# Spreading the softmax reciprocals across partitions on TensorE instead of through DRAM, with the low-half cast moved earlier on GpSimd

## The reference, cut to what matters

```
q = (x @ Wq).reshape(B, S, N_HEADS, HEAD_DIM).transpose(0, 2, 1, 3)
k = (x @ Wk).reshape(B, S, N_KV_HEADS, HEAD_DIM).transpose(0, 2, 1, 3)
v = (x @ Wv).reshape(B, S, N_KV_HEADS, HEAD_DIM).transpose(0, 2, 1, 3)
q = q * cos + _rotate_half(q) * sin
k = k * cos + _rotate_half(k) * sin
q = q * xscale
k = k * (1.0 / xscale)
scores = jnp.einsum('bhqd,bhkd->bhqk', q, k) / scale
scores = jnp.where(causal[None, None], scores, -jnp.inf)
attn = jax.nn.softmax(scores, axis=-1)
out = jnp.einsum('bhqk,bhkd->bhqd', attn, v)
return out @ Wo
```

## Time and profile before

| | us |
|---|---|
| median of 3 runs | 757.99 |
| lowest, highest | 755.96, 760.92 |
| the profiled execution, device time | 760.92 |
| its span, first to last instruction | 758.1 |

### The profile page before, as it was taken

One profiled execution on the slowest core, in us unless ns is written; L12 is line 12 of the kernel. 1 busy time (PEld: TensorE's weight loads), 2 busy tenths in 40 slices (PEclk: granted clock), 3 DMA queues, 4 the chain that ended last, 5 costly groups with the idle time before them and its releaser, 6 DMA issues.

```text
span 758.1 us, 16144 instructions
## 1 busy us (share of the span) xinstructions
PE 610.7 (81%) x4354; PEld 395.9 (52%) x4355; DVE 539.3 (71%) x1555; ACT 468.7 (62%) x1269; POOL 529.3 (70%) x396
## 2 busy tenths in 40 slices
PE   3567749787988888898879888888776799999992
PEld 1244425444555555555545555555453577777761
DVE  6967749877888787888878888788755254333378
ACT  3685456656768576686765867658574674555542
POOL 4574657988787787877878678797988893554510
PEclk9988979999999999999999999999997799999996
DMA  9366966658465574655756557565688773665773
GB/s 306 93 139 157 225 165 140 118 130 182 101 129 125 114 149 101 132 118 117 142 108 125 119 118 140 114 133 116 112 160 189 217 145 73 145 139 138 194 289 106
DMA packets 251448, 109.29 MB, mean 144 GB/s; under 512 B 213556, under 2 KB 236564, under 8 KB 251412
## 3 DMA queue, kind: packets, MB, share of 16 engines
q1 hardware_dynamic: 247300, 98.32, 59.9%
q0 software_dynamic: 3840, 10.52, 4.6%
q10 hardware_dynamic: 272, 0.02, 0.0%
HBM read 41.49 MB, written 19.09 MB: 80 GB/s over the span
## 4 chain that ended last, share of the span: by engine, by line
POOL 20%; PE 19%; DMA 16%; issue 15%; ACT 10%; SPq 10%; DVE 9%; ACTq 1%; POOLq 0%; DVEq 0%
DMA stage<-rinv_dram 10%; PE bank L1591 9%; POOL stage L604 8%; PE bank L1621 6%; POOL arena L590 4%; SPq L471 4%; ACT arena L844 4%; SPq L473 3%; ACT stage L864 3%; DMA arena<-stage 3%; POOL arena L597 3%; DVE bank L1174 2%; PE bank L1600 2%; SPq L477 2%; POOL compare L646 2%
## 5 line engine op out<-in xcount | busy, mean ns | idle before, releaser
L604 POOL TENSOR_TENSOR stage<-arena,stage 128x1280 bf16<-128x1280 f32 x64 | 167.3, 2614 | 10.2 <-DMA arena<-stage 8.5
L844 ACT ACTIVATE arena<-bank,nmax 128x384 f32<-128x384 f32 (+2 forms) x320 | 147.1, 475 | 32.1 <-DVE nmax L1161 31.7
L597 POOL TENSOR_TENSOR arena<-arena 128x512 bf16<-128x512 f32 x80 | 92.3, 1161 | 99.0 <-ACT arena L829 98.9
L1457 PE MATMUL bank<-arena 128*128 128x512 f16 (+7 forms) x768 | 120.9, 308 | 23.8 <-POOL arena L597 21.9
L1426 PE MATMUL bank<-xnT_hi,arena 128*128 (+1 forms) x320 | 114.7, 401 | 29.3 <-DVE arena L1148 25.6
L1487 PE MATMUL bank<-arena 128*128 (+2 forms) x768 | 104.1, 286 | 34.3 <-DVE arena L1152 27.4
L1471 PE MATMUL bank<-arena 128*128 128x512 f16 (+7 forms) x768 | 119.1, 306 | 6.3 <-DMA arena<-stage 6.3
L1161 DVE CUSTOM_DVE_ANT_0 bank<-bank,mask_b 128x512 f32<-128x512 f32 (+3 forms) x256 | 119.3, 524 | 0.0
L1487 PEld LDWEIGHTS bank<-arena 128*128 (+2 forms) x768 | 77.6, 102 | 67.2 <-issue 27.4
L1174 DVE TENSOR_TENSOR bank<-bank,stage 128x512 f32<-128x512 f32 x64 | 68.9, 1077 | 56.9 <-DMA stage<-rinv_dram 55.2
L590 POOL TENSOR_TENSOR arena<-arena 128x512 f32<-128x512 f32 x77 | 98.3, 1286 | 10.6 <-DVE arena L1148 10.3
(11 more groups left out here) (146 smaller groups left out, 1102.3 us busy)
## 6 DMA issues: line engine op xcount, KB each, us to landing
stage<-rinv_dram SPq DMA_DIRECT2D x64, 256.0 KB, 3.4
xs_dram<-s_sb SPq DMA_DIRECT2D x12, 516.0 KB, 5.1
stage<-w_gate_up SPq DMA_DIRECT2D x16, 352.0 KB
arena<-ys_dram SPq DMA_DIRECT2D x8, 512.0 KB, 6.7
stage<-w_down SPq DMA_DIRECT2D x16, 176.0 KB
stage<-wq SPq DMA_DIRECT2D x4, 512.0 KB, 7.5
stage<-wo SPq DMA_DIRECT2D x4, 512.0 KB, 7.7
arena<-stage SPq DMA_TRANSPOSE x128, 3.5
```

What stands on the lines that cost most here:

```text
L597: pool.tensor_tensor(dst, rot_a[buf], hi, ALU.subtract).then_inc(rot_lo, 1)
L604: pool.tensor_tensor(p_lo, probs[par], p_hi, ALU.subtract).then_inc(probs_lo, 1)
L844: return act.activation(dst, src, ACT.Exp, scale=-1.0, bias=nmax[:, par, qt:qt + 1], accum_out=rsum[:, par, to:to + 1])
L1457: ins = pe.matmul(score_bank[u][:, col:col + n_k], qT[a][:, j * S + qt * P:j * S + (qt + 1) * P], kT[m][:, 0:n_k], start=(n == 0), stop=(n ...
```

## The change

The reciprocals no longer go through DRAM. TensorE transposes each of their four columns, broadcast over 128 columns, against the identity into a PSUM bank of its own (`rinv_bank`, bank 4), which leaves all 512 reciprocals in every partition; ScalarE copies the bank to the one buffer `inverse`; `scale_output` then reads bank and buffer with stride one. The two DMAs of a head and their waits are gone from SyncE. `invert_sums` moves into the rope, behind its first product. `p_lo` becomes two buffers, so `low_probs` waits for the transposition two heads back. On GpSimd `low_probs` moves ahead of the rotation's low half, for head 3 also ahead of the sum of k, and for head 0 ahead of the low half of q2; the low half of k moves behind the loop over heads.

```diff
-        p_hi, p_lo = halves[0].bitcast(F16), halves[1].bitcast(BF16)
-        inverse = [stage[:, KEPT + PCOLS + n * S:KEPT + PCOLS + (n + 1) * S] for n in range(2)]
+        p_hi, p_lo = halves[0].bitcast(F16), [half.bitcast(BF16) for half in halves[1:]]
+        inverse = stage[:, KEPT + 3 * PCOLS // 2:KEPT + 3 * PCOLS // 2 + S]
...
-            def load_inverse(rd, j):
-                h = rd.head(j)
-                sp.wait_ge(rinv_out[j % 2], rd.landed(j))
-                if h == 0:
-                    sp.wait_ge(w_lo, W_FIRST)
-                if h >= 2:
-                    sp.wait_ge(o_scaled, h - 1)
-                sp.dma_start(inverse[j % 2], rinv_dram[j % GH:j % GH + 1, :].to_broadcast([P, S])).then_inc(inverse_in[j % 2], 16)
...
                 sp.dma_start_transpose(pT[par][0].rearrange("p (g t) -> p g t", t=P), p_hi).then_inc(hi_in[par], 16)
-                sp.wait_ge(inverted, h + 1)
-                sp.dma_start(rinv_dram[j % GH].rearrange("(p q) -> p q", q=QT), rinv[:, j % GH, :]).then_inc(rinv_out[par], 16)
-                if h > 0:
-                    load_inverse(rd, j - 1)
                 sp.wait_ge(probs_lo, h + 1)
...
             def low_probs(rd, j):
                 h, par = rd.head(j), j % 2
                 pool.wait_ge(probs_hi, h + 1)
-                if not isinstance(h, int) or h >= 1:
-                    pool.wait_ge(lo_in[1 - par], rd.landed(j - 1))
-                pool.tensor_tensor(p_lo, probs[par], p_hi, ALU.subtract).then_inc(probs_lo, 1)
+                if not isinstance(h, int) or h >= 2:
+                    pool.wait_ge(lo_in[par], rd.landed(j) - 16)
...
+                pool.tensor_tensor(p_lo[par], probs[par], p_hi, ALU.subtract).then_inc(probs_lo, 1)
...
+                    low_probs(rd, j + 1)
                     if j == 2 and not rd.last:
                         rotate_sum("k", rd.item("k"))
...
-                    if j == 2 and not rd.last:
-                        rotate_lo("k", rd.rot("k"))
-                    low_probs(rd, j + 1)
...
                 if not rd.last:
+                    rotate_lo("k", rd.rot("k"))
                     rotate_sum("q2", rd.item("q2"))
...
+                    low_probs(rd, GH)
                     rotate_lo("q2", rd.rot("q2"))
-                    low_probs(rd, GH)
...
+            def spread_inverse(rd, j):
+                h = rd.head(j)
+                act.wait_ge(spread_ps, h + 1)
...
+                    act.wait_ge(o_scaled, h)
...
+                act.copy(inverse, rinv_bank[:]).then_inc(spread, 1)
...
                     exponentials(rd, j + 1)
+                    if j > 0 or not rd.first:
+                        spread_inverse(rd, j - 1)
...
                     rotate_hi("k", rd.rot("k"))
+                spread_inverse(rd, 2)
                 output_hi(rd, 2)
...
                 dve.tensor_tensor(rot_a[buf], ps[:], tab[:, cos, :], ALU.mult)
                 half = DH // 2
+                if inverted_head is not None:
+                    invert_sums(*inverted_head)
...
-                dve.wait_ge(inverse_in[j % 2], rd.landed(j))
+                dve.wait_ge(spread, rd.head(j) + 1)
                 dve.wait_ge(pv, rd.head(j) + 1)
-                o = o_bank[j % 2][:].rearrange("d (q p) -> d q p", q=QT)
-                dve.tensor_tensor(o, o, inverse[j % 2].rearrange("d (p q) -> d q p", q=QT), ALU.mult).then_inc(o_scaled, 1)
+                dve.tensor_tensor(o_bank[j % 2][:], o_bank[j % 2][:], inverse, ALU.mult).then_inc(o_scaled, 1)
...
+            def spread_inverse(rd, j):
+                h = rd.head(j)
+                pe.wait_ge(inverted, h + 1)
+                if not isinstance(h, int) or h >= 1:
+                    pe.wait_ge(spread, h)
+                for qt in range(QT):
+                    ins = pe.transpose(rinv_bank[:, qt * P:(qt + 1) * P], rinv[:, j % GH, qt:qt + 1].to_broadcast([P, P]), ident_f[:])
+                ins.then_inc(spread_ps, 1)
...
                     score(rd.head(j + 1), j + 1, queries[j + 1], None, True)
+                    if j > 0 or not rd.first:
+                        spread_inverse(rd, j - 1)
...
                     project(rd, "q2")
+                spread_inverse(rd, 2)
```

More of the change, by code:

```diff
@@ L257, in build @@
         stage = sb("stage", [P, ERING * WE], F32)
-        halves = [stage[:, KEPT + n * (PCOLS // 2):KEPT + (n + 1) * (PCOLS // 2)] for n in range(2)]
-        p_hi, p_lo = halves[0].bitcast(F16), halves[1].bitcast(BF16)
-        inverse = [stage[:, KEPT + PCOLS + n * S:KEPT + PCOLS + (n + 1) * S] for n in range(2)]
+        halves = [stage[:, KEPT + n * (PCOLS // 2):KEPT + (n + 1) * (PCOLS // 2)] for n in range(3)]
+        p_hi, p_lo = halves[0].bitcast(F16), [half.bitcast(BF16) for half in halves[1:]]
+        inverse = stage[:, KEPT + 3 * PCOLS // 2:KEPT + 3 * PCOLS // 2 + S]
         shared_s = [sb("shared_hi", [P, SHARED_W], F16), sb("shared_lo", [P, SHARED_W], BF16)]
@@ L319, in build @@
         bank = [ctx.enter_context(nc.psum_tensor(f"bank{n}", [P, 512], F32)) for n in range(8)]
-        score_bank, o_bank, misc_bank = bank[0:3], [bank[3], bank[5]], bank[6:8]
+        score_bank, o_bank, rinv_bank, misc_bank = bank[0:3], [bank[3], bank[5]], bank[4], bank[6:8]
         gu_bank, hT_bank, y_bank = bank[0:2], bank[2:4], bank[4:6]
@@ L471, in transpose_probs @@
                 sp.dma_start_transpose(pT[par][0].rearrange("p (g t) -> p g t", t=P), p_hi).then_inc(hi_in[par], 16)
[L472 to L475 removed]
                 sp.wait_ge(probs_lo, h + 1)
[L477 removed]
+                sp.dma_start_transpose(pT[par][1].rearrange("p (g t) -> p g t", t=P), p_lo[par]).then_inc(lo_in[par], 16)
             xs_tiles = xs_dram.rearrange("(t p) d -> p t d", p=P)
@@ L601, in low_probs @@
                 pool.wait_ge(probs_hi, h + 1)
-                if not isinstance(h, int) or h >= 1:
-                    pool.wait_ge(lo_in[1 - par], rd.landed(j - 1))
-                pool.tensor_tensor(p_lo, probs[par], p_hi, ALU.subtract).then_inc(probs_lo, 1)
+                if not isinstance(h, int) or h >= 2:
+                    pool.wait_ge(lo_in[par], rd.landed(j) - 16)
+                if isinstance(h, int) and h == 1:
+                    pool.wait_ge(w_lo, W_FIRST)
+                pool.tensor_tensor(p_lo[par], probs[par], p_hi, ALU.subtract).then_inc(probs_lo, 1)
             rotate_lo("q0", PROLOGUE.rot("q0"))
@@ L966, in _ @@
             round_(Round(NG - 1, "last"))
+            spread_inverse(EPILOGUE, -1)
             output_hi(EPILOGUE, -1)
@@ L1167, in invert_sums @@
                 dve.wait_ge(totalled, h + 1)
+                if not isinstance(h, int) or h >= GH:
+                    dve.wait_ge(spread_ps, h + 1 - GH)
                 dve.reciprocal(rinv[:, j, :], rsum[:, par % 2, 0:QT]).then_inc(inverted, 1)
             def scale_output(rd, j):
-                dve.wait_ge(inverse_in[j % 2], rd.landed(j))
+                dve.wait_ge(spread, rd.head(j) + 1)
                 dve.wait_ge(pv, rd.head(j) + 1)
-                o = o_bank[j % 2][:].rearrange("d (q p) -> d q p", q=QT)
-                dve.tensor_tensor(o, o, inverse[j % 2].rearrange("d (p q) -> d q p", q=QT), ALU.mult).then_inc(o_scaled, 1)
+                dve.tensor_tensor(o_bank[j % 2][:], o_bank[j % 2][:], inverse, ALU.mult).then_inc(o_scaled, 1)
             def output_lo(rd, j):
@@ L1187, in add_projection, with first_rope @@
                                   ALU.add).then_inc(misc_free, 1)
-            def first_rope(name, freed=None):
-                rotate_products(name, PROLOGUE.item(name), PROLOGUE.bank(name), freed, ROT_BUF_PROLOGUE)
+            def first_rope(name, freed=None, inverted_head=None):
+                rotate_products(name, PROLOGUE.item(name), PROLOGUE.bank(name), freed, inverted_head, ROT_BUF_PROLOGUE)
             dve.wait_ge(tab_in, 16)
@@ L1228, in round_, with rope @@
                     freed["q0"], freed["k"] = PROLOGUE.rot("q0"), PROLOGUE.rot("q2")
-                def rope(name):
+                def rope(name, inverted_head=None):
                     if not rd.last:
-                        rotate_products(name, rd.item(name), rd.bank(name), freed[name])
+                        rotate_products(name, rd.item(name), rd.bank(name), freed[name], inverted_head)
+                    elif inverted_head is not None:
+                        invert_sums(*inverted_head)
                 for j in range(GH - 1):
@@ L1241, in round_ @@
                             first_rope("q3", PROLOGUE.rot("q1"))
-                        rope("q0")
+                        rope("q0", (h, j + 1))
                         if not rd.first:
@@ L1251, in round_ @@
                             x_items_lo(rd, X_BEFORE[j])
-                        rope(("q0", "q1", "k")[j])
+                        rope(("q0", "q1", "k")[j], (h, j + 1))
                         if not rd.first:
@@ L1281, in round_ @@
                     tile_experts(1)
-                rope("q3")
-                if not rd.last:
```

(2 more changed lines are left out.)

16 lines of the change are left out of this document (7 added, 9 removed).

## The result

| | before | after |
|---|---|---|
| median, us (runs side by side on one chip, 4 of each) | 758.06 | 777.80 |
| lowest, highest | 755.96, 760.92 | 776.34, 781.62 |
| profiled execution; its span | 760.92; 758.1 | 778.42; 776.6 |
| mean granted TensorE clock | 0.946 | 0.938 |
| read from HBM, MB | 41.49 | 24.72 |

The ratio of after to before is 1.0266, with a 95% interval of 1.0212 to 1.0319: slower by 2.7%. The forecast was 763, its range ended at 774. The DMA work did go away, and the time rose all the same.

The account below looks back on a forecast made before the run. No engine is full; a chain of handovers bounds the round. Rounds 0 to 3 -2.5, rounds 4 to 13 +10, round 14 +0.2, round 15 -2.6: +5.1, on the median 763 us; range 740 to 774.

Parts of the forecast that it names:

- a, row maximum 0 to 1: VectorE in a loop round: the reciprocal inside the rope makes it stand 0.5, so 4.93 becomes 5.4 us.
- b, row maximum 1 to 2: VectorE: ScalarE's copy comes when the DMA did; `scale_output` saves 0.4, the reciprocal 0.1; 8.83 becomes 8.3 us.
- c, to `p_lo` 2: Row maximum 2 to `p_lo` 2 on GpSimd: no rotation or landing ahead, 6.36 becomes 4.8 us, 1.6 won.
- d, `p_lo` 2 to the end of low k: GpSimd runs without waits; low q0 (1.1) and `p_lo` 3 (2.6) added ahead of the keys, 9.77 becomes 13.5 us.
- e, to the next row maximum 0: From low k's end: row maximum 0 follows the scores without the wait for DRAM, 1.05 instead of 2.15 us.
- Rival 2: TensorE's clock halves at head 0's scores each round after 2.2 idle: +6.5 to +15, say 773 us; chance 0.12.
- rounds 0 to 3: Opening rounds: 4.0 won in round 1, 1.5 lost in rounds 1 to 3; net -2.5, bounds -4.0 and +3.
- The 4.0 of round 1: Start of round 1: loads leave SyncE some 8 us earlier, so ScalarE's 4.02 stand for a transposition is won.
- rival 3: The early gain does not come, transpositions still queue behind the loads: +4 on the forecast, 767 us; chance 0.07.
- round 14 and the end: Round 14: GpSimd's extra casts lie in slack, +0.2. Round 15: earlier `p_lo` 1 and expert loads, -2.6.
- Rival 1: GpSimd's longer queue finds slack, TensorE's own list sets a round of 30.8: 740 us; chance 0.24.
- Rival 4: Handovers are 1 us a round shorter in all than added up: 753 us, within 1%; chance 0.09.

Follow-up runs that it names:

- the first experiment: The changed kernel with the low half of head 3's probabilities back behind the low half of k on GpSimd, all rounds but the last: 743.66 us, ratio 0.9784.
- the slots' run: The changed kernel with GpSimd's expert slots of round 2 moved behind the low half of k: 776.16 us, ratio 1.0218.

## Why the prediction was wrong, point by point

**The five pieces of a round**, forecast against round 11 of after:

| piece | forecast | after | with the clock kept |
|---|---|---|---|
| a, row maximum 0 to 1 | 5.4 | 6.61 | 5.52 (filler) |
| b, row maximum 1 to 2 | 8.3 | 8.17 | 8.17 |
| c, to `p_lo` 2 | 4.8 | 450.48 - 445.68 = 4.80 | |
| d, `p_lo` 2 to the end of low k | 13.5 | 463.93 - 450.48 = 13.45 | |
| e, to the next row maximum 0 | 1.05 | 464.93 - 463.93 = 1.00 | |
| round | 33.05 | 34.03 | 32.88, 32.95, 32.96 |

**What held.** Four of five pieces within 0.15, and the sum within 0.2 for rounds whose clock stays up: the filler run, the doubled transposes, and three rounds of the slots' run. The DMA's wait did have another behind it, in (b) the sums inside the rope (0.81) beside ScalarE's copy. The copy comes when the DMA did (5.13 against 5.34), `scale_output` is at 0.70, the transposes at 0.43 and free, and the keys are late by GpSimd's list and nothing else. That last one the first experiment shows by its opposite, 30.81. The Trainium skill (TensorE: Matmul & The Clock Gate, Part 4: PE-mode transpose) has some 275 ns for one transpose, and the trace agrees as long as one is timed by itself. The groups after read:

```profile
L1482 PE MATMUL bank<-ident_f,rinv 128*128 128x128 f32 x256 | 40.9, 285 | 10.1 <-ACT stage L859 10.1
```

285 ns each, but they overlap: what a set of four takes from the engine is 0.43, not four times that. The row of before, was the right price.

**First step that failed: the clock, priced as a rival at 0.12 instead of carried in the sum.** Rival 2 named the mechanism, the place and nearly the size: "the first unit comes 0.65 later and the rest up to 1.5". Measured it is 1.1 a round, and in all ten rounds. They rose by 19.8 instead of 10, so +9.9: ten times 1.1 for the clock, less 0.1 a round by which the other pieces came out shorter. Round 14 has +0.9. The trace of before had more to say than the two rows shown. Of its ten waits in front of the opening scores of rounds 5 to 14, 0.64 to 1.96 long, nine kept the clock and one of 1.96 lost it, while three of 1.95 kept it; the 2.02 ahead of round 15 lost it. The forecast of 2.2 idle (measured 2.04) lay beyond every one that had kept it at this place, so a chance of 0.12 was too low; but that all ten would be hit could not be read from the lengths. And a fall in before cost almost nothing:

```profile
317.15 2.89 PE L1457 MATMUL bank<-arena 128*128 128x512 f16 x12 [1.96 <-POOL arena L597]
```

Row maximum 1 came 5.02 after row maximum 0 there instead of 4.93: row maximum 0 stood behind the wait for the DMA, so the projection had time to catch up. After the change row maximum 0 follows the scores directly, and a fall costs 1.1. The price also fell elsewhere than said. From round 8 on, row maximum 0 comes no later (e is 1.00); in rounds 4 to 7 up to 0.3 of the price lies ahead of it. The rest is the projection of q3 behind the scores, at half clock, on which the rope and row maximum 1 wait.

**Second: rounds 0 to 3, forecast -2.5, measured +1.1.** The 4.0 of round 1 did come (4.2), and the run with `p_lo` 3 back gave it up, so rival 3 is out. What failed is "rounds 1 to 3 lose as the loop does, about half each, 1.5 in all". The start up to round 1 lost 1.3, and round 3 won 0.5. Round 2 alone lost 4.6: 1.9 for the slots, which the move of low k left standing ahead of it, and some 2.1 for the stands inside the ropes, if they cost there what they did in the run that took them away. The rest, 0.6, is not traced. Counting every step that the moved instruction passes would have shown the slots.

**Third: round 14 and the end.** Round 14 was +1.1 for +0.2, the clock again (33.98 is a loop round like the others). The end was -3.6 for -2.6, of the right sign; which wait gave the extra 1.0 was not looked into by a run.

**The sum again.** Forecast +5.1. Add 3.6 for rounds 0 to 3, 9.9 for the clock in the loop, 0.9 for round 14, and take off 1.0 at the end: +18.5, the difference of the spans.

**The other rivals.** Rival 1 (GpSimd's list finds slack, 740) did not hold: there is no stand from `p_lo` 2 to low k. Its inner number, 30.8 where TensorE's list sets the round, met the 30.81 of the run with `p_lo` 3 back: TensorE is busy 28.6 of it and stands 2.0 in front of two steps, both for VectorE. That is in part luck, since taking the reciprocals out of VectorE's ropes shortened the same round to 30.34; TensorE's list alone did not set it. Rival 4, shorter handovers, would have a round near 32; the shortest with this order is 32.85.

**What stays open.** Whether the 30.34 us round needs the way over TensorE, or the kernel before would get it from the better order alone, was not measured. Nor was what doubled transposes cost in that fastest version, where TensorE waits only some 0.56 for the keys, nor the reciprocals alone in the kernel after.

## What to carry to other kernels

Ask of each step that is moved what it now stands ahead of, by name, down to the rounds that carry extra work; here one 2.6 us subtraction ahead of the keys was worth some 35 us with the clock's part in it, and 2 us of slot arithmetic nobody had in mind 1.9, where the way over TensorE for 64 broadcast reads was worth 5.4 in the old order. When a forecast has TensorE standing some time before work on the chain, look for the nearest waits in the trace at both levels of the clock and, if the forecast wait is longer than one that lost it, carry the cost in the sum with a weight. Ask too what stands right behind the slowed work, since the same fall cost 0.1 before and 1.1 after. And when removing a DMA makes a kernel slower, look at what was moved with it before you discard it: the same change with the low half of head 3 and the slots behind the keys and the reciprocals behind the ropes is 4% faster than the kernel before. How much of that 4% is owed to the removed DMA is not measured.

## What the runs showed of the hardware that was not expected

- The clock's level after a wait is not decided by its length alone: 2.04 us in front of the same scores kept 2.4 GHz in three loop rounds of one run and lost it in the seven between them. In the kernel after the longest such wait, 2.37 ahead of round 15, kept it (scores at 566.13, 1.79 long), and in before one of 1.96 (scores at 317.15) lost it. The waits of 1.60 to 1.62 (doubled transposes) and 0.64 to 1.07 (filler) all kept it. What else decides it was not tested; in the kernel after the opening scores get shorter from round to round, 3.08 in round 4 and 2.14 in round 14, so the fall comes a little later in each.
- Adding work to an engine can shorten the kernel: six filler matmuls in each wait -12 us, 256 further transposes -11 us. In both the loop round is 1.1 shorter, nearly all of it between row maximum 0 and 1, and its clock is at 1.00. The Trainium skill (TensorE: Matmul & The Clock Gate, Part 4: PE-mode transpose) says that a transpose doesn't count for the clock as other work does. No run here can tell: with doubled transposes the clock held, but they also moved the work behind them later, so the wait fell from 2.04 to 1.62, and that alone may have kept it.
- After the fall the clock was back within the same round: the projection from 432.24 issued at 0.43, and the next one, at 438.02, at 0.22.
